# Which engine adds the products of a dynamic convolution in tiles 8 and 9: VectorE's additions in PSUM start one tile later, GpSimd takes more

## What is computed

```python
x = x + conv(_ln_c(x), reduce_w, reduce_b, span_w, span_b)
    # h = reduce_w x + b;  kern = span_w h + b   (49 weights per pixel and group)
    # out = (kern * patches).sum(axis=3)
t = _to_tokens(x)
t = t + ffn(_ln_t(t), router_w, w1, w2, w3)
    # gates: softmax of the two highest of 8;  silu(w1 t) * (w3 t), then w2
```

## Time and profile before

| | |
|---|---|
| median of 3 runs | 1479.97 us (1479.87 to 1483.39) |
| the profiled execution's own time | 1478.88 us |
| its span | 1477.1 us |
| tiles 0 to 27 | to 1182.6 us of the span |
| expert blocks alone | from there to the end |
| VectorE busy | 1118.9 us (76%) |
| GpSimd busy | 1082.3 us (73%) |
| TensorE busy | 1249.0 us (85%) |
| mean granted TensorE clock | 0.95 of full |

### The profile page before, as it was taken

How to read it: one execution, slowest core, us unless ns; L and a number is a source line. 1 busy time by engine, 2 the same in 40 slices (tenths; PEclk the granted TensorE clock), 3 DMA queues, 4 the chain that set the end, 5 groups by cost and what they waited for, 6 DMA issues and landing times. The chain is left out here.

```text
span 1477.1 us, 23321 instructions
## 1 busy us (share of the span) xinstructions
PE 1249.0 (85%) x7763; PEld 1025.3 (69%) x7763; DVE 1118.9 (76%) x1663; ACT 579.2 (39%) x1961; POOL 1082.3 (73%) x781
## 2 busy tenths in 40 slices
PE   6899898978979998999898999889989887677771
PEld 4677777766867777777776787777777766465661
DVE  7999989989898988888889898888889944122220
ACT  5344333323444533544344443344533253223330
POOL 5767787755886878687787787877778875665665
PEclk9999999989999999999999999999999899899996
DMA  4111111121242322433224333143332455666652
GB/s 126 61 42 53 56 58 59 57 72 57 40 103 65 92 56 56 100 86 77 55 56 104 83 77 79 36 98 85 70 79 30 102 146 124 159 150 130 144 114 25
DMA packets 93347, 120.42 MB, mean 82 GB/s; under 512 B 11531, under 2 KB 72428, under 8 KB 93082
## 3 DMA queue, kind: packets, MB, share of 16 engines
q1 hardware_dynamic: 53802, 90.97, 20.4%
q0 software_dynamic: 39424, 27.96, 13.6%
HBM read 78.92 MB, written 42.65 MB: 82 GB/s over the span
## 5 line engine op out<-in xcount | busy, mean ns | idle before, releaser
L864 DVE TENSOR_TENSOR prod<-kern_ps,xn 128x896 f32<-128x896 f32 x592 | 627.2, 1082 | 50.0 <-PE kern_ps L598 47.0
L598 PE MATMUL kern_ps<-h_stack,span 98*128 98x448 f32 x1372 | 467.3, 425 | 106.8 <-DVE prod L864 66.2
L1111 POOL TENSOR_TENSOR acc_p<-acc_p,prod 128x896 f32<-128x896 f32 x180 | 411.9, 2289 | 81.6 <-DVE prod L864 78.2
L1132 POOL DMA_INDIRECT out<-y_tok,idx x224 | 351.7, 1570 | 136.0 <-issue 65.9
L613 PE MATMUL acc_ps<-ident_sb,prod 128*112 128x128 f32 x2960 | 399.6, 279 | 0.0
L613 PEld LDWEIGHTS acc_ps<-ident_sb,prod 128*112 128x112 f32 x2960 | 351.0, 136 | 38.8 <-DVE x L1069 7.8
L598 PEld LDWEIGHTS kern_ps<-h_stack,span 98*128 98x128 f32 x1372 | 225.8, 199 | 196.0 <-DVE prod L864 111.0
L1120 POOL DMA_INDIRECT xs<-rows_x,slots x224 | 218.5, 976 | 58.5 <-issue 36.8
L546 PEld LDWEIGHTS bank<-w2b,hid 114*128 114x128 f32 x1344 | 181.9, 202 | 50.7 <-DVE xf_lo L1062 26.0
L546 PE MATMUL bank<-w2b,hid 114*128 114x128 f32 x1344 | 190.2, 288 | 26.3 <-DVE xf_lo L1062 15.9
L795 ACT ACTIVATE silu<-h_ps 114x512 f32<-114x512 f32 x132 | 78.9, 598 | 233.7 <-PE h_ps L639 233.6
(11 more groups left out here) (157 smaller groups left out, 1337.3 us busy)
## 6 DMA issues: line engine op xcount, KB each, us to landing
wb<-wexp SPq DMA_DIRECT2D x56, 684.0 KB, 5.3
xb<-xs SPq DMA_DIRECT2D x56, 264.0 KB, 3.3
w2b<-in_w SPq DMA_DIRECT2D x56, 171.0 KB
xt<-in_x SPq DMA_DIRECT2D x28, 224.0 KB, 3.8
out<-x SPq DMA_DIRECT2D x28, 224.0 KB, 2.8
wexp<-wb SPq DMA_DIRECT2D x8, 684.0 KB
xs<-rows_x,slots POOLq DMA_INDIRECT x224, 2.4
out<-y_tok,idx POOLq DMA_INDIRECT x224
```

The source lines that it names most:

```text
L598: last = mm(kern_ps[:, g % 2, i, 0:N], span[:, k * C:(k + 1) * C], h_stack[:, t % 2, :], start=True, stop=True)
L864: v.tensor_tensor(pair_rows(dst), kern.rearrange("p i (r w) -> p i r w", w=W), taps, ALU.mult).then_inc(s_prod, 1)
L1111: g_.tensor_tensor(acc_p[:], acc_p[:], prod[:, (t * TAPS + u) % PRING, :], ALU.add).then_inc(s_padd, 1)
L1132: g_.indirect_dma_start(out=out, out_offset=bass.IndirectOffsetOnAxis(ap=idx[:, b % XBRING, q:q + 1], axis=0), in_=y_tok[:, b % 2, q * C:( ...
```

## The change

```diff
-LATE = 8
-BY_POOL = [tuple(range(0, 21, 2)) if t < 2 else (0, 2, 5, 7, 10, 12, 15, 17, 20) if t < LATE else tuple(range(0, 22, 3)) for t in range(TILES)]
+LATE = 9
+BY_POOL = [tuple(range(0, 21, 2)) if t < 2 or t == 8 else (0, 2, 5, 7, 10, 12, 15, 17, 20) if t < LATE else
+           (0, 2, 4, 6, 8, 11, 12, 15, 18, 21) if t == 9 else tuple(range(0, 22, 3)) for t in range(TILES)]
```

## The result

| | before | changed |
|---|---|---|
| median of 20 runs | 1479.7 us (1477.0 to 1484.4) | 1485.1 us (1478.4 to 1492.5) |
| ratio | | 1.003, 95% interval 1.0019 to 1.0042 |
| span of the profiled execution | 1477.1 us | 1483.5 us |

The change is slower by 0.3%. 6.5 us less were forecast, and the range ended at 1479.5.

A forecast was written before the change was run, and what follows sets the result against it. VectorE was taken to set tile 8, with excess waits in tile 9's first third. -4.4 - 1.6 - 0.5 = -6.5 us took 1478.88 to 1472.4, or 1473.5 us for the median; range 1469 to 1479.5.

The forecast's parts named there:

- VectorE sets tile 8, and four pairs less are 4.4 us less.: Tile 8: four multiply-and-add pairs on VectorE become plain multiplications, 4 x 1.10 = 4.4 us less.
- Does it keep up?: GpSimd in tile 8: falls behind by nearly the whole 8-slot ring but just keeps up; three more additions cost nothing.
- GpSimd's chain, the scatter, the load, `mx`, unit 4: Tiles 8 to 9: last addition ends 321.5, scatter starts 316.0, load lands 322.7, `mx` ends 323.2, unit 4 6.0 us earlier.
- the wait on the load: Start of tile 9: TensorE, there at about 321, waits some 1.5 us for block 0's load before `mx`.
- GpSimd gets two additions, into 11.6 us of waits: nothing.: Tile 9: two more GpSimd additions, 4.5 us, fit into its 11.6 us of waits for products and cost nothing.
- Slots 0 to 17 two steps earlier: nothing in sum, and no end of the range.: Blocks before block 3: same matmuls in the same program, only earlier; costed at nothing.
- The clock: TensorE's lower 1.2 GHz level may leave tile 9's start or shift in later tiles; 2.5 us allowed to either side.
- the one that ended slower: Tiles 8 and 9: GpSimd sets both, its five added additions on the path, +6.9 us, 1486.9; chance 0.07.
- its signs: Tile 8's last GpSimd addition ends later than 327.5, and GpSimd's waits in tile 9 are gone.
- the 1.6 and 0.5 us put to tile 9's start: Tile 9: 1.6 us off VectorE's 2.10 us wait behind unit 3, 0.5 us off the 1.20 us wait at 339.13.

The follow-up runs named there:

- the relief: Table `ge` also written to PSUM, so L997 and L1010 read one input there; on the kernel before 1461.5 us (0.9871), with tile 9's list alone 1458.6 us (0.9856).

## Why the prediction was wrong

- *VectorE sets tile 8, and four pairs less are 4.4 us less.* The work is right: 33.0 to 28.8 us busy. The time is not: alone, tile 8's table gave 0.09% (1.3 us; from 3.7 less to 1.0 more). In the changed kernel's trace 2.5 us arrived in the tile, since GpSimd's fuller queue brought a wait that wasn't costed. "Does it keep up?" was asked for the products and the scatter alone. The `rsqrt` in the same queue, late by 2.5 us, has waiters too, and VectorE waits 1.9 us for them. Tile 11 was longer too, at the lower clock, but the table of tile 8 isn't shown to be why: it reads 46.6 us with that table alone, 46.8 with the scatter places alone and 46.3 with tile 9's list alone.
- *GpSimd's chain, the scatter, the load, `mx`, unit 4:* right, each within 0.4 us, but for the wait on the load, which didn't show. Unit 4 came 6.4 us earlier (6.0).
- *"GpSimd gets two additions, into 11.6 us of waits: nothing."* This step failed. The time was free for GpSimd, but not for VectorE: the addition of product 11 falls on L998. Alone the list costs 0.16% (0 to 0.33%, so barely clear of nothing), and with the relief nothing can be measured. The meeting itself is shown, with 1.7 and 1.2 us too many in L998 and L1011 of tile 9.
- *"Slots 0 to 17 two steps earlier: nothing in sum, and no end of the range."* This step failed too, and was the larger of the two: 0.26% (0.11 to 0.41%) by itself, nothing that can be measured once the slots are held. The count of matmuls is the same, but slot 8 crossed into the last step of tile 9 (0.7 us of waiting more), and other work of tiles 10 and 11 changed places with it; the forecast read only tile 9's start. How the rest of the cost comes about stays open.
- *The clock:* 2.5 us to either side, put to the start of tile 9. That start did keep its full clock. The lower clock came behind the stall instead, in the tile's middle, and in tile 11.
- *The rivals:* the one that ended slower had GpSimd's additions on the path as a queue. Its time, 1486.9, is near the 1485.1 measured, but its signs stayed away: GpSimd's last addition ended at 322.2 and not behind 327.5, and in tile 9 it still waited 9.8 us for products. It was another mechanism: in tile 9 GpSimd was not late, VectorE stood still beside it.
- Parts measured alone, against before: -0.09, +0.26 and +0.16%, each to about 0.16 either way, +0.33 in sum, and the change has +0.30. Against the forecast that is 3.1 us missing in tile 8, 3.8 too many by the slots and 2.4 by the list; the 1.6 and 0.5 us put to tile 9's start may be in the last two already (in the traces tile 9 is 2.4 us shorter with the scatter places alone, 0.9 longer with the list alone), so they aren't counted again.

## What to carry to other kernels

Before additions are moved to GpSimd because it has time to spare, list the instructions of VectorE that read two tensors in SBUF and ask what will run beside each. A small instruction that reads ten times its usual length and ends with one of another engine is the thing to look for in a trace of before; here it was worth more than the change. And a table entry that moves other tables (here the scatter places, by `LATE`) is costed by where its steps land and by what other places move with them, not by the count of its work.

## What was not expected of the hardware

- An instruction of VectorE of 0.15 to 0.2 us with two inputs in SBUF took up to 2.6 us beside an addition of GpSimd and ended 0.02 to 0.06 us after it. The same instruction with one input in PSUM took 0.14 to 0.19 in all tiles. Where a subtraction of VectorE with two inputs in SBUF began first, it kept its 0.86 and the addition took 2.64 or 2.67 us for 2.10.
- Such a stall can cost more than its length: with 1.9 us less of VectorE's time tile 13 was 3.7 us shorter, and TensorE, which had fallen to 1.2 GHz 0.6 us behind the stall, no longer did.
- L862, L865 and the other large instructions of VectorE, with one input in PSUM and one in SBUF, kept their 1.07 to 1.10 us beside GpSimd's additions.
